# Cross attention and FFN on one core: keys made already transposed, their roots multiplied onto the scores, and head 3's scores first

## What is computed

```python
# x: 16 batches x 100 queries x 512; context: 16 batches x 361 keys x 256; 16 heads of 128
q = rmsnorm((layernorm(x) @ Wq).reshape(B, Sq, H, D), gq)
k = rmsnorm((ctx @ Wk).reshape(B, Skv, H, D), gk)    # rmsnorm(k) = k * rsqrt(mean(k*k) + eps) * g
scores = einsum('bqhd,bkhd->bhqk', q, k) / sqrt(D)
attn = softmax(scores, axis=-1)
out = einsum('bhqk,bkhd->bqhd', attn, v)             # v = ctx @ Wv, taken as (attn @ ctx) @ Wv
x = x + out.reshape(B, Sq, H * D) @ Wo
```

## Time and profile before

| | us |
|---|---|
| three timed runs | 1964.23, 1964.02, 1962.70 |
| their median | 1964.02 |
| profiled execution, its own time | 1964.5 |
| profiled execution, span in the trace | 1962.7 |

### The profile page before, as it was taken

How to read it: one execution, slowest core, us unless ns; L and a number is a source line. 1 busy time by engine, 2 the same in 40 slices (tenths; PEclk the granted TensorE clock), 3 DMA queues, 4 the chain that set the end, 5 groups by cost and what they waited for, 6 DMA issues and landing times.

```text
span 1962.7 us, 33387 instructions
## 1 busy us (share of the span) xinstructions
PE 1941.3 (99%) x11276; PEld 1850.4 (94%) x11276; DVE 1586.2 (81%) x2990; ACT 983.1 (50%) x2275; POOL 1074.4 (55%) x1211
## 2 busy tenths in 40 slices
PE   8999999999999999999999999999999999999999
PEld 7899899999999999999999999988999999999999
DVE  6888877787877787887878887888888888888875
ACT  4655555555555455555545543444444444444442
POOL 5755555412423322334222335888888888878871
PEclk9999999999999999999999999999999999999999
DMA  6434443433433333333223333211111111111101
GB/s 212 135 120 156 161 139 116 134 100 91 132 113 96 124 101 114 102 120 118 94 95 116 114 101 109 66 33 44 33 33 33 33 33 33 33 33 33 33 1 68
DMA packets 93512, 174.53 MB, mean 89 GB/s; under 512 B 13264, under 2 KB 49760, under 8 KB 91296
## 3 DMA queue, kind: packets, MB, share of 16 engines
q1 hardware_dynamic: 93344, 172.39, 27.2%
HBM read 139.00 MB, written 33.36 MB: 88 GB/s over the span
## 4 chain that ended last, share of the span: by engine, by line
PE 88%; DVE 5%; POOL 3%; issue 2%; ACT 1%; DMA 1%; SPq 0%; DVEq 0%; ACTq 0%; POOLq 0%
PE psum L420 43%; PE psum L794 19%; PE psum L451 6%; PE psum L484 4%; PE psum L508 4%; PE psum L514 3%; PE psum L509 3%; PE psum L493 3%; PE psum L524 1%; PE psum L569 1%; POOL inter_lo L1981 1%; PE psum L575 0%; DVE ysum L1497 0%; DVE g L1464 0%; DVE work L1347 0%
## 5 line engine op out<-in xcount | busy, mean ns | idle before, releaser
L1838 POOL TENSOR_SCALAR k_ss<-k_ss 122x4 f32<-122x4 f32 x192 | 37.2, 194 | 423.3 <-DVE k_ss L1300 423.2
L899 ACT ACTIVATE work<-psum,stats,q_rstd 100x361 f32<-100x361 f32 x256 | 163.8, 651 | 177.6 <-DVE stats L1338 177.6
L1244 DVE TENSOR_TENSOR kaT_lo<-psum,kaT_hi 128x488 fp32r<-128x488 f32 (+2 forms) x384 | 214.1, 613 | 45.2 <-ACT kaT_hi L842 45.1
L420 PE MATMUL psum<-wk,ctxT_hi 128*122 128x512 f32 x768 | 242.0, 396 | 0.0
L1981 POOL TENSOR_TENSOR inter_lo<-g,inter_hi 128x400 fp32r<-128x400 f32 x127 | 143.1, 1132 | 126.1 <-ACT inter_hi L842 125.3
L842 ACT CAST kaT_hi<-psum 128x488 fp32r<-128x488 f32 (+2 forms) x384 | 178.7, 540 | 57.9 <-PE psum L493 57.8
L1840 POOL TENSOR_TENSOR k_ss<-k_ss,power 122x4 f32<-122x4 f32 x192 | 193.9, 1010 | 16.0
L420 PE MATMUL psum<-inter_hi,down_hi 128*128 128x400 f32 x512 | 176.1, 344 | 3.2 <-POOL inter_lo L1981 1.6
L1330 DVE TENSOR_REDUCE stats<-psum 100x2 f32<-100x722 f32 x128 | 115.9, 905 | 75.0 <-PE psum L451 75.0
L420 PE MATMUL psum<-inter_lo,down_hi 128*128 128x400 f32 x512 | 175.5, 343 | 0.0
L420 PE MATMUL psum<-inter_hi,down_lo 128*128 128x400 f32 x512 | 175.3, 342 | 0.0
(11 more groups left out here) (260 smaller groups left out, 5939.5 us busy)
## 6 DMA issues: line engine op xcount, KB each, us to landing
head_w<-spill_sq SPq DMA_DIRECT2D x48, 512.0 KB, 3.5
head_w<-spill_so SPq DMA_DIRECT2D x46, 512.0 KB, 3.8
wk<-spill_sk SPq DMA_DIRECT2D x12, 1024.0 KB, 4.9
wv<-spill_sv SPq DMA_DIRECT2D x48, 256.0 KB, 2.8
spill_so<-head_w SPq DMA_DIRECT2D x16, 512.0 KB, 3.0
spill_sq<-head_w SPq DMA_DIRECT2D x14, 512.0 KB, 3.0
wk_raw<-in_ctxT SPq DMA_DIRECT2D x12, 361.0 KB, 4.2
spill_sk<-wk SPq DMA_DIRECT2D x4, 1024.0 KB, 6.0
```

What stands on the lines that cost most here:

```text
L420: last = e.matmul(out, a_, b_, start=begins and i == 0, stop=ends and i == len(passes) - 1)
L899: e.activation(attn[h][:, 0:SKV], bank[3 + h][0:SQ, 0:SKV], ACT.Exp, bias=st[:, h:h + 1], scale=rq[:, i * QH + h:i * QH + h + 1], accum_ou ...
L1244: e.tensor_tensor(dst, src, high.bitcast(F32), ALU.subtract).then_inc(S[sem], 1)
```

## The change

Keys are made transposed at once: `keys(u, h)` has `wk` of one head as the stationary side (128 x 128) and the context's 362 columns moving, six matmuls for each of four heads, into banks 0, 1, 2 (heads 0 to 2) and 7 (head 3). Key transposes, `key_sums` and `normalise_keys` are gone. The keys are split without having been normalised. Their roots reach the scores in another way:

1. ScalarE squares each head (`square_key`), TensorE sums the 128 rows by `keys_summed(u, 7)` (four strip matmuls, L540), ScalarE takes the result to `k_sums` (four rows of use, partitions 0, 32, 64, 96).
2. SP gathers these into `k_root` (124 partitions of 12 numbers, pieces of 48 B), GpSimd makes the roots (`key_rstd`, one multiply-add and one power), SP stores them in DRAM and loads them back spread to 100 partitions (`spread_roots`: 100 rows of 1,488 numbers, 595 KB).
3. VectorE multiplies the scores by this `key_root` and the query's root in one operation that also takes the maximum (`scaled`, `tensor_tensor_reduce`), writes them to SBUF and then negates the maximum; the exponential reads SBUF.

The order moves too. Head 3's scores come first in the unit, before the next keys, and have buffers of their own (`k3T`, two). The next keys are made in the order 3, 0, 1, 2, or 0, 1, 2, 3 where `key_order` says so: for the units after an odd unit of quads 1 to 14, after units 0 and 4, and after six units with `i = 0` (u = 12, 24, 28, 40, 44, 56). Then come the scores of heads 0 and 1, `keys_summed`, the scores of head 2. The products of query, value and output steps are laid anew between these; `squares_summed` stands behind `keys_summed`. Head weights are reloaded in three parts around the gather, the store and the spread.

The core of the diff:

```diff
+            def keys_summed(u, into):
+                e.wait_ge(S["ksq"], 4 * u + QH)
+                e.wait_ge(S["kTl"], 4 * u + 1)
+                for h in range(QH):
+                    last = e.matmul(bank[into][cols(h, STRIP), 0:SCOLS], strip[:, :], k_sq[:, h, :], start=True, stop=True)
+                last.then_inc(S["kss"], 1)
...
             for u in range(UNITS - 1):
-                scores(u)
-                for t in range(KT):
-                    keys(u + 1, t)
+                scores(u, 3)
+                for n, h in enumerate(key_order(u + 1)):
+                    keys(u + 1, h)
...
+                scores(u, 0)
+                scores(u, 1)
+                keys_summed(u + 1, 7)
+                if i == 3 and more and quad > 0:
+                    e.wait_ge(S["mx"], 4 * u + 1)
+                    squares_summed(quad + 1, 6)
+                scores(u, 2)
...
-                for t in range(KT):
-                    transpose_keys(u + 1, t)
...
+            def key_hi(u, h):
+                if h < QH - 1 and u > 0:
+                    e.wait_ge(S["y"], 2 * u)
+                elif u > 1:
+                    e.wait_ge(S["sc"], 4 * (u - 2) + 1)
+                hi(keys_of(u, h, 0), key_bank(h), "kTh")
...
+                for h in key_order(u + 1):
+                    square_key(u + 1, h)
+                    if h == 3:
+                        key_hi(u + 1, h)
+                exponential(u, 3)
+                exponential(u, 0)
+                key_sums_evicted(u + 1, 7)
+                exponential(u, 1)
...
                 attended(u, 0)
                 if norm1_at(u, 0) is not None:
                     norm_hi(norm1_at(u, 0), 5)
+                key_hi(u + 1, 0)
+                key_hi(u + 1, 1)
+                key_hi(u + 1, 2)
                 attended(u, 1)
...
+                e.tensor_tensor_reduce(out=attn[h][:, 0:SKV], in0=bank[3 + h][0:SQ, 0:SKV], in1=key_root[:, h * SPAN:h * SPAN + SKV],
+                                       scale=rq[:, at:at + 1], scalar=LOWEST, op0=ALU.mult, op1=ALU.max,
+                                       accum_out=st[:, h:h + 1]).then_inc(S["mx"], 1)
+                e.wait_ge(S["mx"], 4 * u + RANK[h] + 1)
+                e.tensor_scalar(st[:, h:h + 1], st[:, h:h + 1], -1.0, None, ALU.mult).then_inc(S["neg"], 1)
...
+                key_lo(u + 1, 3)
+                scaled(u, 3)
+                scaled(u, 0)
+                scaled(u, 1)
+                normalise_attn(u, 3)
+                scaled(u, 2)
+                normalise_attn(u, 0)
+                normalise_attn(u, 1)
+                normalise_attn(u, 2)
...
+            def gather_sums(u):
+                e.wait_ge(S["ksv"], u + 1)
+                load(k_root[:, :], k_sums[0:(QH - 1) * STRIP + 1:STRIP, :], "d_kr")
+
+            def store_roots(u):
+                e.wait_ge(S["krs"], u + 1)
+                load(d["kr"], k_root[:, :], "d_kd")
+
+            def spread_roots(u):
+                e.wait_ge(S["d_kd"], 16 * (u + 1))
+                if u > 0:
+                    e.wait_ge(S["mx"], 4 * u)
+                load(key_root[:, :], d["kr"].rearrange("p n -> (p n)").unsqueeze(0).broadcast_to([SQ, QH * SPAN]), "d_kb")
```

More of the change, by code:

```diff
@@ L799, in tensor_program @@
             last = (NG - 1) * GB
-            scores(u)
+            for h in ORDER:
+                scores(u, h)
             half(0, 1, 0)
@@ L1075, in scalar_program @@
                     norm2_copy(norm2_at(u - 1), 6)
-                if i == 3 and more:
-                    squares_evicted(quad + 1, 3)
+                if u == GB - 1:
+                    squares_evicted(1, 7)
+                elif quad > 0 and more and i == 0:
+                    query(quad + 1, 0, 7)
+                elif quad > 0 and more and i == 2:
+                    query(quad + 1, 3, 7)
             u = UNITS - 1
             square(0)
-            for h in range(QH):
+            for h in ORDER:
                 exponential(u, h)
@@ L1393, in vector_program @@
             ln1_lo(3, 6)
[L1394 to L1395 removed]
+            key_lo(0, 3)
             e.wait_ge(S["d_gq"], 16)
@@ L2381, in sync_program @@
                     load_wk(quad + 2)
+                if u + 1 < UNITS:
+                    gather_sums(u + 1)
+                reload_used(u, 1)
+                if u + 1 < UNITS:
+                    store_roots(u + 1)
+                reload_used(u, 2)
+                if u + 1 < UNITS:
+                    spread_roots(u + 1)
+                if i == 0 and quad >= NQUAD:
+                    for h in range(QH):
+                        reload_wv(4 * quad + h)
+                for n in late_splits(u):
+                    store_head(n)
+                    load_head(FRESH_PLACE[n] + 2)
                 for n in value_splits(u):
@@ L2384, in sync_program @@
                     load_wv(n + 2)
-                for n in used_in(u):
-                    if n + 2 not in FRESH_PLACE and n + 2 < len(ITEMS):
-                        reload_head(n + 2)
                 if u == 1:
```

606 lines of the change are left out of this document (297 added, 309 removed).

## The result

| | before | changed |
|---|---|---|
| median of four interleaved runs | 1963.74 us | 2055.47 us |
| their range | 1962.70 to 1964.23 | 2048.53 to 2059.40 |
| profiled execution, own time | 1964.5 | 2058.93 |
| its span in the trace | 1962.7 | 2057.1 |

The ratio is 1.0464 (95%: 1.0430 to 1.0498). The sign was forecast, the size was not: +35 us against +92, and 2055.5 is above the range, whose end was 2028.

A forecast was written before the change was run, and what follows sets the result against it. TensorE, busy for all 600 us of the stage, was taken to bound the kernel, so waits count in full. 1964.5 - 40.5 + 38 + 26 + 12 = 2000.0, put at 1999.5 us for the median; range 1950 to 2028.

The forecast's parts named there:

- TensorE's work: Key matmuls and transposes replaced by the new keys and sums: -0.6 us a unit, -40.5 us in all.
- The chain at `keys_summed`: TensorE waits 0.56 us for head 3's square, cast and low part where its keys are made last, 36 times.
- The transposes in i = 1: Attention transposes wait 0.55 us for VectorE's four `scaled` and four normalisations in units with i = 1.
- Bank 6: Head 3's scores at the unit's head wait directly for bank 6's last users, norms included: +26 us.
- The DMA chain: Gather, GpSimd root, store and spread with hops take 11.6 us per unit, ends 10 and 17.
- Rival A: Every link in the waiting chains is 0.15 us shorter, so waits shrink by 50 us: 1950 us; chance 0.20.
- Rival C: `scaled` takes 0.85 us: +22, 2021 us, chance of this dear case 0.08; at 0.65: -8, 1992 us.
- Rival B: The spread is late, the transfer chain being 14.4 us instead of 11.6: about +28, 2028 us; chance 0.12.
- The transfers per unit: Gather, store and spread in each unit are hidden with 1.3 us to spare: 0 us.
- The start: Unit 1's gather stands behind the context loads on SP, delaying unit 0's transposes and all behind: +12 us.
- In units with head 3 first: Low part done 3 us earlier, attention transposes have 0.3 us of slack: no wait added.
- +18 for the two waits behind `keys_summed`: Attention transposes wait for VectorE, +12 us; output or value step waits for `k_sums`, +6 us.

The follow-up runs named there:

- experiment 7: Changed kernel with the norm's copy and casts ahead of the next unit's key casts on ScalarE and VectorE, in units with a norm: 2023.87 us.
- Experiment 3: Changed kernel with dummy transposes filling TensorE's waits in unit 1, before head 3's scores at v = 6 and 10, and before the v = 12 query step: 2048.79 us.
- experiment 8: Changed kernel with unit 1's gather, store and spread ahead of context loads N2 and N3, and those loads behind the spreads of units 2 and 3: 2043.96 us.
- Experiment 1: Changed kernel without gather, GpSimd root, store and spread; `key_root` filled with ones, sums and `scaled` kept: 2031.76 us.
- experiment 2: Changed kernel with unit 1's gather, store and spread ahead of context loads N2 and N3 on SP: 2051.39 us.
- Experiment 5: Changed kernel without VectorE's negation of the maximum; the exponential takes the maximum with its own sign: 2035.66 us.
- Experiments 4: Changed kernel with `keys_summed` behind the scores of head 2 instead of ahead of them: 2061.23 us.
- 6: Changed kernel with head 3's keys made first in every unit: 2061.21 us.
- experiment 12: Changed kernel without the roots and their transfers, and without `keys_summed` and its eviction; bank 7 waits only for what it needs: 2027.28 us.

## Why the prediction was right in sign and wrong in size

The waits that the sum had are there, for the reasons given and nearly at the size given. What failed is what the sum left out or set too low: no term for the clock (measured 17.5 us), 0 for late transfers (about 13) and +12 for the start (about 23).

**Right.** *The bound*: TensorE with no slack, so that waits count in full. *TensorE's work*: -36.5 for -40.5, with 0.58 a unit for 0.6 in the units that could be taken clean. *The chain at `keys_summed`*: 0.65 where I had 0.56, in 37 units for 36, released by the row that I named. *The transposes in i = 1*: 0.54 where I had 0.55. *Bank 6*: 27.4 for 26; experiment 7 shows the cause, a copy behind three casts. *`scaled`*: 0.70 for 0.72. *The DMA chain* of a unit: 11.6 in both, though with a spread of 5.5 instead of 3.8, and gather and store quicker than my 2.4. Rival A (links shorter by 0.15) falls: every link has its full length. Rival C falls with 0.70. Rival B has the right mechanism in the wrong form: the chain is not 14.4 everywhere, it is 11.6 in most units and, with the gather's excess added, 14.5 to 18.6 in five.

**Wrong, in the order of size.**

1. *No term for the clock.* The sum priced waits at their length. Behind 11 of the longer ones TensorE ran 3.4 us or more at half clock, 17.5 us between 80 and 1240 us, and at the start 20.5 us stand at half clock, of which TensorE worked in the last 8. Experiment 3 takes 12.9 of the 17.5 away without shortening a wait, experiment 7 about 14. The time also scatters with the clock, by 11 us over four runs against 1.5 before: the two slower had a granted clock of 0.983 and 0.984, the two faster 0.986 and 0.987.
2. *"The transfers per unit ... so hidden, by 1.3 us: 0".* A median against a cover of 1.3 us was the wrong comparison; what counts is the worst gather, 8.95 us behind a 1 MB reload of `wk`. Five units, 13 us with what follows, of which some 4, near 239 us, are absent from other traces (experiment 8).
3. *"The start: +12, bounds 8 and 14".* It was about 23. The issue of the gather came within 3 us of the forecast; the gather behind the context loads took 7.2 instead of 2.4, and half clock came on top. Experiment 1 (14.7 up to unit 3) shows that the transfers cause it; 2 and 8 show that SP's order sets where the wait falls, and recover 0 and 5.5 us of it. My upper bound held nothing for a DMA that queues behind others. The prediction also said that the context loads wait for their buffers; they stand behind no such wait, yet every load of 117 rows holds SP, here and before.
4. *"In units with head 3 first ... 0.3 us of slack: nothing"* and +18 for the two waits behind `keys_summed`, where 22 came. The slack held while the roots were in time. In eight such units VectorE waited 1.9 to 4.1 us for the spread, or in unit 60 for GpSimd's root of the queries, and the transposes then waited 0.25 to 1.3 us (units 8, 16, 52 and 60 of i = 0; 10, 18, 34 and 50 of i = 2). The seven units of i = 0 with head 3 last wait 0.70. Experiment 5 shows VectorE's chain as the releaser.
5. *Small terms.* The wait at `keys_summed` was 4 us larger and the work saved 4 us smaller than forecast. The working of the latter does not add up either: its own terms give 5.52 - 4.905 = 0.615 a unit and 41.7 in all, not 40.5.

**Where the work saved went.** The change took 171 us of VectorE's work and 36 of TensorE's, and the kernel became no shorter, since the new order ties TensorE several times a unit to a chain over two in-order engines: `k3T_lo`, `scaled`, the exponential, the normalisation. Experiments 4, 6 and 12 take a wait or work out of TensorE's queue and nearly all of the time reappears at another place; 5 and 7 shorten or reorder what the other engines do, and the time falls. What stays open: some 4 us of the 94.4, why a clock stretch stands behind some of the longer idles and not behind others, and how far VectorE's chain could be shortened with the negation kept or folded into another operation, for which no kernel was made.

## What to carry to other kernels

Where TensorE is busy for the whole stage, a wait on it can cost more than its length, because its clock may fall behind it; here 11 of 20 waits of over 1 us cost some 1.5 us more. Work saved on the bounding engine is worth little if a chain of the others closes up behind it (4.5 of 85 us in experiment 12): before one counts it, the lag of those engines at each semaphore is to be worked out, and the cheapest gains are then in the order of their queues (experiment 7: 32 us from six moved calls). A transfer with a deadline is judged by its worst neighbour in the queue, not by its median.

## What the runs showed that I had not expected

- A gather of 6 KB in 124 pieces takes 1.98 us as a median, up to 4.9 in some others, and 4.9 to 8.95 in the five units behind loads of 800 KB, 1 MB or weights.
- Each of the 16 context loads of 117 rows holds SP, for 3.3 to 7.4 us in the changed kernel (5.7 and 7.4 at the start) and for 4.3 and 5.3 us at the start of experiment 2; the load of 244 rows directly ahead of each takes 0.25 to 0.31. Everything behind them on the queue pays. The two always come as a pair, so it is not shown which of them is the cause.
- The spread of 581 KB to 100 partitions takes 5.5 us, slower than the loads of 512 KB to 128 partitions (3.6 in this trace). The Trainium skill (DMA: Bandwidth & Descriptors, Anatomy of one DMA) gives a fixed part and a rate over all engines; by it the spread would be an estimated 3.4. But the same page of the Trainium skill (Why a DMA increments its semaphore by 16 and not by 1) has 100 partitions served by ten of the sixteen engines, by which the estimate is 4.2. In the trace the quickest spread took 4.1 and the median 5.5; which engines it used is not shown.
- Half clock follows 11 of 20 idle times of over 1 us (the 11 are of 1.2 to 2.9 us), for 3.4 us each and once for 6.8.
